# A decoder layer on one core: the order of evictions in the first batch, and centring in two parts

## The chip, the cores and the metric

The kernel runs on one core of a Trainium2 chip. The metric is the device time in microseconds (us) of one execution; the median of three runs of the kernel before is 1821.55 us (1820.07 to 1822.1). The engines are TensorE (PE, matrix products), VectorE (DVE), ScalarE (ACT), GpSimd (POOL) and SyncE (SP), which here only issues DMA transfers. Each engine works through its own list of instructions in order; they wait for each other by semaphores.

## The reference

Eight batches of 512 tokens of 512 values each (`x`), with a context of the same shape:

```python
x = x + attn(layernorm(x), queries, combiners)              # heads of 128, no softmax
x = x + xattn(layernorm(x), ctx, ctx, Wq,bq, Wk,bk, Wv,bv)  # softmax attention over the context
x = x + ffn(layernorm(x), router, experts, shared mlp)      # 16 experts, top 2, capacity 640
```

The first attention has no softmax, so `out_h = X_h @ (Q_h . (X^T X) . C)`: with `G = X^T X`, a 512x512 matrix per batch, the kernel forms `T = G C`, `M = Q T` and `A = X M`. In the cross attention Wq and Wk are multiplied once (`W = Wq Wk^T`), so scores are `(y1 W) ctx^T`; values are `V = ctx Wv`.

## The kernel before, in words

Phase 1 does both attentions batch by batch, phase 2 the shared MLP and the experts. The change touches phase 1 only (`phase1`, from L108). Work is cut into named steps, and one list `order` (L1244 to L1275) gives for every iteration i the steps of batches i and i+1 in the order in which every engine goes through them: Y1T, V (values), ST0, LN0, MEAN, STORE, LN2, Q, Y2, G, T, SC (scores), M, PT (turned probabilities), C (context), A, LN1, PV. Iteration -1, which begins the kernel, has a list of its own (L1257). Each engine has a `step(name, b)` that issues its part of a step. Where an engine has no part, the step's place in the list says nothing for it.

Most products are made in three passes (`three_pass`, L63): each operand is split into a high part (a copy rounded by ACT) and a low part (the difference, by DVE or POOL), and high-high, high-low, low-high are summed: 12 matmuls of 128x512 for one output tile. Tiles stand in the 8 PSUM banks by the table BANK (L123). `filled` waits until PE has filled a bank; `drained` waits until a bank's eviction is done (semaphores `s_ev`), which for a split product is DVE's instruction.

First batch, up to batch 0's Q. W is made in four columns (INIT to INIT3, L1026); for each, ACT copies the high part into WH (L599) and DVE makes the low part (L794). C: ACT copies the context's four chunks to `ch` (L672, shown at the helper's line L527), DVE makes `cl` (L805), for b = 0; for later batches POOL makes it (L469). M: four times eight matmuls, ACT evicts (L570). A: 32 matmuls of 128x128 (L1145) in four tiles, in banks 6, 7, 0, 1; DVE evicts each at L831 and adds x. Then DVE takes statistics (L735), deviations (L724 to L753), and ACT normalises to y (L532, step LN1). V: four tiles of 12 matmuls (L72) in banks 5, 6, 7, 4. V's group waits at L1038 to L1043 before its first tile: for the last W bank, for `cl`, and for the third eviction of A (`drained(pe, "A", b, 2)`). ACT copies each tile to `vh` (`value_hi`, L688), DVE makes `vl` (`residual`, L843, at L846). Y1T: PE turns y (L1007), ACT copies to `y1h` (L604), DVE makes `y1l` (L885). Q: four tiles (L72), in the same banks as V, whose first tile waits for `y1l` chunk by chunk, and whose tile c waits for V's tile c. Step KEY (POOL L457, ACT L582, then two small transfers by SP) makes a row that DVE uses at L765 behind Y1T; ST0(1) and LN0(1) follow, and G(1) on PE waits for them.

Centring. For each batch `centre` (L296) takes the tokens' means from the turned tokens `xT`, in four instructions (L303), one for each chunk; each waits for `s_xT` (the load) and `s_mrow` (the row of means, written to DRAM and read back, L343 and L351). For batch 0 DVE does it, later POOL, in step MEAN. A(b) waits on PE for all four (L1138). In POOL's list, MEAN(b+2) follows PV(b). In PV(b) POOL adds y2 to x (L480), then for each of four token tiles t copies the two halves of the words of y2 (L491) into one of two buffers, `halves(b, t)`, t modulo 2, so tile 2 waits until the store of tile 0 has landed, and tile 3 for tile 1 (L488). SP stores each (L394) as it is ready, and after all four issues the turning of the first two probability tiles (L400, from `p_planes` that ACT writes), and the load of x (L402). The turned probabilities pass through DVE (L921) and ACT, in step M and PT, and DVE makes their low part (`p_lo`, L783) between the evictions of A; PV's first two tiles on PE wait for it (L1163). ACT copies M behind `p_top`, the first half of one of them (L567). POOL's L469 (step C) runs at that time. DVE's L914, in SC, is an addition of one column between the maximum of a tile of scores (L912) and the bias for its exponential (L648).

Of the kernel before, what the change touches and what calls it, by code (L numbers as in the profile page):

```python
# [40 lines left out]
B, S, D = 8, 512, 512  # L41
# [66 lines left out]
def phase1(nc, ctx, a, Y, shared, at):  # L108
# [123 lines left out]
        return y1_words[:, :, t * P:(t + 1) * P].bitcast(U16).rearrange("p c (n two) -> p c n two", two=2)  # L232

    ph, pl = y1h, y1l
    P_BY_DMA = 2
    p_planes = [at(44 + t, [2, D], U16) for t in range(P_BY_DMA)]
    p_turned = [at(row, [2 * NC, P], U16) for row in (12, 43)]
# [55 lines left out]
    s_ct_hi, s_ct_lo, s_ct_stored, s_ct_loaded = (sem(f"s_ct_{k}") for k in ("hi", "lo", "stored", "loaded"))  # L293
    s_g_hi = sem("s_g_hi")

    def centre(eng, b):  # L296

        eng.wait_ge(s_xT, 16 * (b + 1))
        eng.wait_ge(s_mrow, 16 * (b + 1))
        by_tile = mean_row[:].rearrange("q (p t) -> q t p", t=NT)  # L300
        for c in range(NC):
            tokens = xT[:, c, :].rearrange("q (t p) -> q t p", t=NT)
            eng.tensor_tensor(tokens, tokens, by_tile, ALU.subtract).then_inc(s_centred, 1)  # L303

# [101 lines left out]
    def gpsimd(pool):  # L406
# [39 lines left out]
        def step(name, b):  # L446
            if name == "MEAN":
                if b >= 1:
                    centre(pool, b)
            if name == "FILL":  # L450
                pool.wait_ge(s_small, 16 * 3)
                fill_tables()
# [18 lines left out]
            if name == "PV":  # L471
                if b == 0:
                    pool.wait_ge(s_pad, 32)
                if b < B - 2:
                    pool.wait_ge(s_stat[0], b + 3)
                else:
                    drained(pool, "V", b + 1, 0)
                for t in range(NT):
                    pool.wait_ge(s_y2, NT * b + t + 1)
                    pool.tensor_tensor(x[b % XS][:, t, :], x[b % XS][:, t, :], y2[:, t, :],  # L480
                                       ALU.add).then_inc(s_base, 1)
                if b == B - 1:
                    pool.wait_ge(s_ttop, NT)
                    pool.wait_ge(s_tlow, NT)
                for t in range(NT):
                    n = NT * b + t
                    if n >= 2:
                        pool.wait_ge(s_yout[t % 2], 16 * (n // 2))  # L488
                    words = y2[:, t, :].bitcast(U16).rearrange("p (d two) -> p d two", two=2)
                    for half in range(2):  # L490
                        last = pool.tensor_copy(halves(b, t)[:, half, :], words[:, :, 1 - half])  # L491
                    last.then_inc(s_halves, 1)
            if name == "LN1" and b in BY_DMA:
                filled(pool, "PT", b - 1, NT - 1)
                for t in range(NT):
                    pool.wait_ge(s_y1, NT * b + t + 1)
                    words = y[:, t, :].bitcast(U16).rearrange("p (d two) -> p d two", two=2)
                    for half in range(2):
                        last = pool.tensor_copy(y1_planes[t][:, half, :], words[:, :, 1 - half])
                    last.then_inc(s_planes, 1)  # L500
# [24 lines left out]
    def scalar(act):  # L525
# [25 lines left out]
        def step(name, b):  # L551
# [136 lines left out]
            def value_hi(t):  # L688
                filled(act, "V", b, t)
                bank = bank_of("V", b, t)  # L690
                copy(vh[:, t, :], bank[:]).then_inc(s_vh, 1)

            if name == "V" and b in BY_DMA:
                filled(act, "PV", b - 1, NT - 1)
                for t in range(NT):
                    y1_words_of(t)
                    if t >= 1:
                        y1_hi(t - 1)
                    if 0 < t < NT - 1:
                        value_hi(t - 1)  # L700
                y1_hi(NT - 1)
                for t in range(2, NT):
                    value_hi(t)
            else:
                for t in value_tiles(name, b):
                    value_hi(t)
                    if t == 1 and b == B - 1:
                        normalise_x2(b - 1)

# [2 lines left out]
    def vector(dve):  # L712
# [75 lines left out]
        def step(name, b):  # L788
# [60 lines left out]
            if name == "V":  # L849
                if b == B - 1:  # L850
                    for t in value_tiles(name, b):
                        residual(t)
                if b >= 1:
                    key_row_ready(b)
                for t in range(NT - 1):
                    if b >= 1:
                        key_row_and_statistics(b, t)
                if b in BY_DMA:
                    for t in range(2, NT):
                        dve.wait_ge(s_y1_turned[t], 16 * b)  # L860
                        dve.tensor_copy(word_halves(t)[:, :, :, 0], y1_turned[t][:, NC:2 * NC, :])\
                           .then_inc(s_low_dve, 1)
                    for t in range(NT):
                        cols = slice(t * P, (t + 1) * P)
                        dve.wait_ge(s_y1h, NC * b + t + 1)
                        dve.tensor_tensor(y1l[:, :, cols], y1_words[:, :, cols], y1h[:, :, cols].bitcast(F32),
                                          ALU.subtract).then_inc(s_ev["Y1T"], 1)
                        if t == 1:
                            residual(0)
                elif b < B - 1:  # L870
                    residual(0)
                if b >= 1:
                    key_row_and_statistics(b, NT - 1)
                    key_row_bias(b)
                if b < B - 1:
                    for t in range(1, NT):
                        residual(t)
            if name in LATE:
                residual(LATE[name])
            if name == "Y1T" and b not in BY_DMA:  # L880
                for c in range(NC):
                    dve.wait_ge(s_y1h, NC * b + c + 1)
                    y1_filled(dve, b, c)
                    bank = bank_of("Y1T", b, c)
                    dve.tensor_tensor(y1l[:, c, :], bank[:], y1h[:, c, :].bitcast(F32), ALU.subtract)\  # L885
                        .then_inc(s_ev["Y1T"], 1)
            if name == "LOW":
                for q in range(H):
                    dve.wait_ge(s_ct_hi, q + 1)
# [108 lines left out]
    def tensor(pe):  # L998
# [23 lines left out]
        def step(name, b):  # L1022
# [13 lines left out]
            if name == "V":  # L1036
                if b == 0:
                    pe.wait_ge(s_wh, NC + 1)  # L1038
                    drained(pe, "W", 0, NC - 1)
                pe.wait_ge(s_cl, NC * (b + 1))  # L1040
                if b not in BY_DMA:
                    drained(pe, "PV", b - 1, 3)
                drained(pe, "A", b, 2)  # L1043
            if name in LATE:
                drained(pe, "Q", b, LATE[name] - 2)
            if name == "V" or name in LATE:
                for t in value_tiles(name, b):
                    if b in BY_DMA and t == NT - 1:
                        drained(pe, "PV", b - 1, 3)
                    cols = slice(t * P, (t + 1) * P)  # L1050
                    parts = [(ch[:, c, cols], cl[:, c, cols], VWH[:, c, :], VWL[:, c, :]) for c in range(NC)]
                    three_pass(pe, bank_of("V", b, t)[:], parts).then_inc(s_mm["V"], 1)
# [121 lines left out]
def phase2(nc, ctx, a, Y, shared, at, attn):  # L1174
# [70 lines left out]
    for i in range(-1, B):  # L1245
# [9 lines left out]
        if i == -1:  # L1255

            steps = [("ST0", 0), ("LN0", 0), ("WV", 0), ("INIT", 0), ("MEAN", 0), ("G", 0), ("INIT1", 0), ("T", 0),  # L1257
                     ("C", 0), ("INIT2", 0), ("M", 0), ("INIT3", 0), ("KEY", 0), ("FILL", 0), ("A", 0), ("LN1", 0)]
            steps.append(("V", 0))
        if i == 0:  # L1260
            steps.remove(("V", 0))
# [461 lines left out]
```

## Time and profile before

| | |
|---|---|
| median of 3 runs | 1821.55 us (1820.07 to 1822.1) |
| the profiled execution's own time | 1821.36 us |
| its span | 1819.6 us |
| PE busy | 1805.0 us, 99% |
| DVE, ACT, POOL busy | 874.2 (48%), 799.2 (44%), 920.4 (51%) |
| granted clock of PE | 0.998 of full speed over the span |
| chain that ended last | PE 96%, DVE 1%, DMA 1% |

The span is the time from the profile's first to its last instruction; the execution's own time has 1.76 us around it. All times below are microseconds from the span's start unless marked ns. In a row of a timeline, several like instructions in a row stand as one, with their count; its second number is the time from the first one's start to the last one's end. Instructions of an engine are pipelined, so the end of one may lie behind the start of the next. `L527` is the helper `copy` of ACT, whatever it copies; `L72` is any product in three passes.

### The profile page before, as it was taken

How to read it: one execution, taken by the hardware profiler on the slowest of the kernel's cores; microseconds unless marked ns; L12 is line 12 of the kernel's file. 1: busy time of each engine (PE TensorE's matmuls, PEld its weight loads, DVE VectorE, ACT ScalarE, POOL GpSimd, SP SyncE). 2: the span in 40 equal slices, each digit the busy share in tenths (PEclk: the TensorE clock that was granted, in tenths of full speed). 3: DMA queues.
4: the chain of work that ended last, by engine and by line, in shares of the span. 5: the costliest groups of instructions: out<-in, count | busy, mean ns of one | idle time of the engine just before them, and what ended most of it. 6: DMA issues, size and time to landing. Idle time of an engine off the chain costs nothing.

```text
span 1819.6 us, 27098 instructions
## 1 busy us (share of the span) xinstructions
PE 1805.0 (99%) x9960; PEld 1598.3 (88%) x9960; DVE 874.2 (48%) x2064; ACT 799.2 (44%) x1574; POOL 920.4 (51%) x808
## 2 busy tenths in 40 slices
PE   9999999999999999999999999999999999999997
PEld 6888888888887878888999999999999999999996
DVE  6668777787745444332444323443343423443242
ACT  4555556555544343332444434444344433444331
POOL 3454564546653232225665656556665556656531
PEclk9999999999999999999999999999999999999999
DMA  8454545443552333224666676666666666666722
GB/s 319 147 133 123 151 140 151 134 141 97 147 114 42 47 54 68 36 41 93 173 140 131 163 155 134 139 146 161 147 140 128 161 152 140 144 134 163 155 31 29
DMA packets 254292, 229.34 MB, mean 126 GB/s; under 512 B 171697, under 2 KB 171697, under 8 KB 252881
## 3 DMA queue, kind: packets, MB, share of 16 engines
q1 hardware_dynamic: 228864, 174.51, 36.2%
q0 software_dynamic: 25296, 53.11, 17.4%
q8 instruction: 79, 1.29, 0.3%
q14 instruction: 53, 0.43, 0.1%
HBM read 138.80 MB, written 49.97 MB: 104 GB/s over the span
## 4 chain that ended last, share of the span: by engine, by line
PE 96%; DVE 1%; DMA 1%; issue 0%; ACT 0%; SPq 0%; POOL 0%; DVEq 0%; ACTq 0%; POOLq 0%
PE ps L72 67%; PE ps L1668 23%; PE ps L1001 4%; PE ps L1145 1%; PE ps L1007 1%; DMA buffer<-means 0%; DMA buffer<-in_x 0%; DMA means<-mean 0%; DVE buffer L831 0%; ACT buffer L1478 0%; DVE buffer L303 0%; PE ps L1081 0%; DVE buffer L783 0%; ACT buffer L527 0%; DVE buffer L794 0%
## 5 line engine op out<-in xcount | busy, mean ns | idle before, releaser
L72 PE MATMUL ps<-buffer,buffer 128*128 128x320 f32 (+1 forms) x6900 | 1239.2, 341 | 1.3 <-DVE buffer L831 0.8
L72 PEld LDWEIGHTS ps<-buffer,buffer 128*128 128x128 f32 x6900 | 1120.9, 188 | 107.6 <-issue 1.5
L1420 POOL TENSOR_TENSOR buffer<-buffer,buffer 128x512 fp32r<-128x512 f32 x289 | 380.4, 1483 | 252.3 <-ACT buffer L1478 252.0
L1668 PE MATMUL ps<-buffer,buffer 128*128 128x512 f32 x1904 | 437.4, 390 | 0.4 <-DVE buffer L1611 0.4
L1668 PEld LDWEIGHTS ps<-buffer,buffer 128*128 128x128 f32 x1904 | 356.0, 188 | 74.3 <-DVE buffer L1611 0.8
L1520 ACT ACTIVATE buffer<-ps 128x320 f32<-128x320 f32 (+1 forms) x240 | 112.5, 469 | 600.1 <-PE ps L72 600.0
L1478 ACT ACTIVATE buffer<-buffer 128x512 fp32r<-128x512 f32 (+1 forms) x491 | 293.2, 651 | 163.1 <-PE ps L1668 91.8
L1586 DVE TENSOR_TENSOR ps<-ps,buffer 128x320 f32<-128x320 f32 (+2 forms) x198 | 100.2, 506 | 488.8 <-ACT buffer L1520 488.8
L1467 POOL DMA_INDIRECT out_tokens<-buffer,slot_list x80 | 125.8, 1573 | 185.5 <-DVE buffer L1616 177.8
L519 POOL DMA_INDIRECT slots<-pairs,slot_u x64 | 63.6, 993 | 181.7 <-DVE slot_u L988 164.7
L527 ACT ACTIVATE buffer<-buffer 128x512 fp32r<-128x512 f32 (+1 forms) x212 | 126.5, 681 | 20.4 <-DMA buffer<-buffer 15.1
L1616 DVE TENSOR_SCALAR buffer<-ps,slot_list 128x512 f32<-128x512 f32 x80 | 59.7, 747 | 112.1 <-PE ps L1668 112.1
L532 ACT ACTIVATE buffer<-buffer,shift,rstd 128x512 f32<-128x512 f32 x96 | 70.3, 804 | 94.5 <-DVE shift L753 94.5
L1570 DVE TENSOR_TENSOR buffer<-ps,buffer 128x320 fp32r<-128x320 f32 (+2 forms) x198 | 96.6, 488 | 10.0 <-ACT buffer L1478 9.0
L1433 POOL DMA_INDIRECT buffer<-tokens_normed,slot_list x80 | 83.5, 1044 | 29.3 <-issue 29.3
L510 POOL TENSOR_TENSOR buffer<-buffer,buffer 128x512 f32<-128x512 f32 x32 | 40.5, 1294 | 103.0 <-DVE shift L753 99.1
L1478 ACT ACTIVATE buffer<-ps 128x320 fp32r<-128x320 f32 (+2 forms) x198 | 86.3, 436 | 0.7 <-DVE ps L1586 0.7
L527 ACT ACTIVATE buffer<-ps 128x512 fp32r<-128x512 f32 (+2 forms) x124 | 63.9, 557 | 44.4 <-PE ps L72 34.0
L1586 DVE TENSOR_TENSOR buffer<-ps,buffer 128x512 f32<-128x512 f32 (+1 forms) x42 | 29.0, 690 | 101.1 <-ACT buffer L1520 101.0
L1554 DVE COPY buffer<-buffer 128x512 uint16<-128x512 uint16 x80 | 73.6, 942 | 0.5
L735 DVE BATCH_NORM_STATS2 stats<-buffer 128x6 f32<-128x512 f32 x96 | 61.0, 680 | 7.8 <-DMA buffer<-in_x 7.7
L469 POOL TENSOR_TENSOR buffer<-buffer,buffer 128x512 fp32r<-128x512 f32 x28 | 38.4, 1403 | 37.7 <-ACT buffer L527 37.7
(131 smaller groups left out, 1090.8 us busy)
## 6 DMA issues: line engine op xcount, KB each, us to landing
buffer<-in_wts SPq DMA_DIRECT2D x289, 256.0 KB, 3.0
buffer<-in_xT SPq DMA_DIRECT2D x8, 1024.0 KB, 5.5
buffer<-in_ctxT SPq DMA_DIRECT2D x8, 1024.0 KB, 8.4
out_tokens<-buffer SPq DMA_DIRECT2D x8, 1024.0 KB, 4.3
tokens_normed<-buffer SPq DMA_DIRECT2D x32, 256.0 KB, 3.1
out_tokens<-buffer POOLq DMA_DIRECT2D x32, 256.0 KB, 6.7
buffer<-in_x SPq DMA_DIRECT2D x7, 1024.0 KB, 5.6
buffer<-combiners_top SPq DMA_DIRECT2D x6, 1024.0 KB, 5.0
```

Source lines behind the costliest of these rows:

```text
L72: last = pe.matmul(out, left, right, start=(c == 0 and i == 0), stop=(c == len(parts) - 1 and i == 2))
L527: return act.activation(dst, src, ACT.Copy)
L1001: last = pe.matmul(out, left, right, start=(i == 0), stop=(i == len(pairs) - 1))
L1420: pool.tensor_tensor(wl[n % RING][:], wraw[n % RAW][:], wh[n % RING][:].bitcast(F32), ALU.subtract).then_inc(s_wl, 1)
L1433: pool.indirect_dma_start(xn[:, t, :], None, Y[:, :], rows_at(groups[g][1], t), bounds_check=N + PAD - 1).then_inc(s_xg, 16)
L1467: pool.indirect_dma_start(out[:, :], rows_at(part, t), ost[:, t, :], None, bounds_check=N + PAD - 1, compute_op=ALU.add).then_inc(s_add[t] ...
L1478: return act.activation(dst, src, ACT.Copy)
L1520: act.activation(silu[u % TMP][0:rows_of(c), 0:n], bank[0:rows_of(c), 0:n], ACT.Silu)\
L1554: dve.tensor_copy(halves_of(t)[:, :, :, 0], xp[t][:, NC:2 * NC, :]).then_inc(s_xlow, 1)
L1570: dve.tensor_tensor(lo[:, first:first + n], product_of(u)[0:rows, 0:n], hh[0:rows, c, first:first + n].bitcast(F32), ALU.subtract).then_in ...
L1586: dve.tensor_tensor(product_of(u)[0:rows_of(c), 0:n], up_bank[u % 2][rows, 0:n], silu[u % TMP][0:rows_of(c), 0:n], ALU.mult).then_inc(s_ht, 1)
L1668: ins = pe.matmul(down_bank[n % 2][:], left, right, start=(c == 0 and i == 0), stop=(c == FC - 1 and i == len(passes) - 1))
```

## The change

Five edits, all in phase 1:

1. In the first list, C(0) moves from behind T(0) to behind M(0). On ACT, the copies of W's third column and of M now come ahead of the context's four; DVE's `cl` come behind the low part of W's third column.
2. PE's V(0) no longer waits for A's third eviction before its first tile; tile t > 0 waits for A's eviction t - 1. (The other condition is rewritten and means the same.)
3. V(0)'s last tile: ACT's copy and DVE's residual move from V(0) to the end of Y1T(0), behind the four copies and four low parts of the turned tokens.
4. POOL's centring of batch b+2, for b = 0 to 5: its first two chunks move into PV(b), behind the copies of halves of tile 1.
5. The other two stay in MEAN(b+2).

```diff
@@ phase1
+    CENTRED_EARLY, CENTRED_LATE = range(2), range(2, NC)
...
-    def centre(eng, b):
+    def centre(eng, b, chunks=range(NC)):
         eng.wait_ge(s_xT, 16 * (b + 1))
         eng.wait_ge(s_mrow, 16 * (b + 1))
         by_tile = mean_row[:].rearrange("q (p t) -> q t p", t=NT)
-        for c in range(NC):
+        for c in chunks:
...
@@ gpsimd step
             if name == "MEAN":
                 if b >= 1:
-                    centre(pool, b)
+                    centre(pool, b, CENTRED_LATE if b >= 2 else range(NC))
...
                     last.then_inc(s_halves, 1)
+                    if t == 1 and b + 2 < B:
+                        centre(pool, b + 2, CENTRED_EARLY)
@@ scalar step
+            if name == "Y1T" and b == 0:
+                value_hi(NT - 1)
...
                 for t in value_tiles(name, b):
-                    value_hi(t)
+                    if (b, t) != (0, NT - 1):
+                        value_hi(t)
@@ vector step
                 if b < B - 1:
-                    for t in range(1, NT):
+                    for t in range(1, NT if b > 0 else NT - 1):
                         residual(t)
...
             if name == "Y1T" and b not in BY_DMA:
...
                         .then_inc(s_ev["Y1T"], 1)
+                if b == 0:
+                    residual(NT - 1)
@@ tensor step
                 pe.wait_ge(s_cl, NC * (b + 1))
-                if b not in BY_DMA:
+                if b == B - 1:
                     drained(pe, "PV", b - 1, 3)
-                drained(pe, "A", b, 2)
+                if b > 0:
+                    drained(pe, "A", b, 2)
...
                         drained(pe, "PV", b - 1, 3)
+                    if b == 0 and t > 0:
+                        drained(pe, "A", b, t - 1)
@@ phase2, the list of steps for i == -1
-                     ("C", 0), ("INIT2", 0), ("M", 0), ("INIT3", 0), ("KEY", 0), ("FILL", 0), ("A", 0), ("LN1", 0)]
+                     ("INIT2", 0), ("M", 0), ("C", 0), ("INIT3", 0), ("KEY", 0), ("FILL", 0), ("A", 0), ("LN1", 0)]
```

## Rows read from the trace of the kernel before

**Rows 1.** page, part 1: busy us, share of the span, instructions

```profile
PE 1805.0 (99%) x9960; PEld 1598.3 (88%) x9960; DVE 874.2 (48%) x2064; ACT 799.2 (44%) x1574; POOL 920.4 (51%) x808
```

**Rows 2.** PE timeline, first batch: start, us, what, [idle before <-who ended it]

```profile
29.11 1.02 PE L1026 MATMUL ps<-buffer,buffer 128*128 128x512 f32 x2
...
30.55 3.84 PE L1145 MATMUL ps<-buffer,buffer 128*128 128x128 f32 x32 [0.42 <-ACT buffer L527]
...
35.21 11.16 PE L72 MATMUL ps<-buffer,buffer 128*128 128x512 f32 x48 [0.82 <-DVE buffer L831]
...
46.22 1.91 PE L1007 MATMUL ps<-ident,buffer 128*128 128x128 f32 x16
...
48.48 11.13 PE L72 MATMUL ps<-buffer,buffer 128*128 128x512 f32 x48 [0.36 <-DVE buffer L885]
```

**Rows 3.** PE timeline, batches 2 to 7

```profile
143.38 32.92 PE L72 MATMUL ps<-buffer,buffer 128*128 128x512 f32 x144
...
198.65 3.81 PE L1145 MATMUL ps<-buffer,buffer 128*128 128x128 f32 x32 [0.72 <-issue]
...
202.21 32.91 PE L72 MATMUL ps<-buffer,buffer 128*128 128x512 f32 x144
...
260.16 32.92 PE L72 MATMUL ps<-buffer,buffer 128*128 128x512 f32 x144
...
376.21 32.94 PE L72 MATMUL ps<-buffer,buffer 128*128 128x512 f32 x144
...
434.18 11.59 PE L72 MATMUL ps<-buffer,buffer 128*128 128x512 f32 x48
```

**Rows 4.** ACT timeline, first batch

```profile
27.34 2.19 ACT L527 ACTIVATE buffer<-buffer 128x512 fp32r<-128x512 f32 x4 [2.03 <-DMA buffer<-in_ctxT]
...
29.44 1.55 ACT L527 ACTIVATE buffer<-ps 128x512 fp32r<-128x512 f32 x3
...
44.14 1.54 ACT L527 ACTIVATE buffer<-ps 128x512 fp32r<-128x512 f32 x3
...
55.81 2.94 ACT L532 ACTIVATE buffer<-buffer,shift,rstd 128x512 f32<-128x512 f32 x4 [1.71 <-DVE shift L753]
```

**Rows 5.** DVE timeline, first batch

```profile
29.41 2.48 DVE L805 TENSOR_TENSOR buffer<-buffer,buffer 128x512 fp32r<-128x512 f32 x4
...
33.01 2.71 DVE L831 SCALAR_TENSOR_TENSOR buffer<-ps,rstd,buffer 128x512 f32<-128x512 f32 x4
...
44.82 1.89 DVE L846 TENSOR_TENSOR buffer<-ps,buffer 128x512 fp32r<-128x512 f32 x3 [1.24 <-ACT buffer L527]
...
47.65 2.48 DVE L885 TENSOR_TENSOR buffer<-ps,buffer 128x512 fp32r<-128x512 f32 x4
```

**Rows 6.** POOL timeline, batches 1 to 7

```profile
183.72 2.28 POOL L491 COPY buffer<-buffer 128x512 uint16<-128x512 uint16 x4
...
189.30 1.17 POOL L491 COPY buffer<-buffer 128x512 uint16<-128x512 uint16 x2 [3.30 <-DMA tokens_normed<-buffer]
...
192.35 6.20 POOL L303 TENSOR_TENSOR buffer<-buffer,buffer 128x512 f32<-128x512 f32 x4
...
376.17 4.35 POOL L469 TENSOR_TENSOR buffer<-buffer,buffer 128x512 fp32r<-128x512 f32 x3 [4.31 <-ACT buffer L527]
...
421.49 2.29 POOL L491 COPY buffer<-buffer 128x512 uint16<-128x512 uint16 x4 [2.71 <-DMA tokens_normed<-buffer]
...
434.14 5.51 POOL L469 TENSOR_TENSOR buffer<-buffer,buffer 128x512 fp32r<-128x512 f32 x4 [4.38 <-ACT buffer L527]
```

**Rows 7.** DVE timeline ahead of the probabilities' product, batches 3, 6, 7

```profile
197.74 1.12 DVE L921 COPY buffer<-buffer 128x512 uint16<-128x512 uint16 x1 [0.55 <-DMA buffer<-buffer]
...
377.43 0.69 DVE L783 TENSOR_TENSOR buffer<-buffer,buffer 128x512 fp32r<-128x512 f32 x1
...
435.52 1.72 DVE L783 TENSOR_TENSOR buffer<-buffer,buffer 128x512 fp32r<-128x512 f32 x1
```

**Rows 8.** line L914: engine op xcount: ns min/median/max, first and last start

```profile
L914 DVE TENSOR_TENSOR mr<-smax,krow x32: 158/506/1391, 66.7 to 475.7; 128x1 f32<-128x1 f32 x32
```

## The prediction

> **What bounds the kernel now.** I read the page first: TensorE (PE) is busy for 99% of the span, so only time in which PE stands still, or work added to it, can move the result [rows 1]. Next the PE timeline of the first batch. A row's bracket is the idle time in front of it and who ended it; the reader is to see three small holes: attention's product A(0) starts at 30.55 with 0.42 of idle behind ScalarE (ACT), V(0) at 35.21 with 0.82 behind VectorE's evictions of A at L831, and, with the transposes of Y1 at 46.22 right behind V, Q(0) at 48.48 with 0.36 behind VectorE (DVE) at L885 [rows 2]. "Idle" understates a hole, since an end in the trace overlaps the next start: the 32 matmuls of A start 35.21 - 30.55 = 4.66 us before V, and without a wait they take 3.6 (from 198.65 to 202.21, 3.56 [rows 3]), so this hole is worth 1.1 us. In the PE timeline of the later batches I compare the starts of the 144-matmul block behind A: 143.38, 202.21, 260.16, and two batches later 376.21 [rows 3]. Steps: 58.83, 57.95, and 116.05 for two. Against 57.95 the step into batch 3 is 0.88 too long and the last pair 0.15 too long. The 0.88 stands in front of A(3), 0.72 of it as idle time at 198.65. Who ended it, the view doesn't say; the GpSimd (POOL) timeline does: its four centring instructions of batch 3 run from 192.35 for 6.20, to 198.55, and A waits for them [rows 6]. They were late because the copies of halves at L491 sat 3.30, and once more, behind stores to DRAM. In the other batches that gap is 2.7, as in the row at 421.49 [rows 6], and the centring is in time. Last the ACT and DVE timelines of the first batch [rows 4, 5], for the durations.
>
> **First batch.** Times are the trace's; a prime marks my estimate.
> M's copy ahead of the context's. Before, ACT makes the four copies of the context from 27.34 for 2.19, and only then the evictions of WH's third column, M and WH's fourth, three from 29.44 at about 0.5 each [rows 4]. PE gives M just ahead of the row at 29.11, so ACT can take M at 29.3', ends it at 29.9', and PE, with two matmuls from 29.11 (0.94 from start to start), starts A(0) at 30.05' in place of 30.55. Gain 0.5 at this point.
> Its cost: the context's copies start at 29.85' in place of 27.34. DVE works without a hole from the first of four L805 at 29.41, 0.62 each, through two L794 to the evictions of A at 33.01 [rows 5]. Now one L794 goes first, to 30.03', then DVE waits until the first copy is there at 30.45', so everything behind it is 0.42 later: L805 ends at 32.9', the last L794 at 33.5', the evictions of A start at 33.43'. Nothing else is moved past ACT here: WH's fourth column is copied at 32.05', before DVE asks for it. POOL's KEY products wait for the last L805 and so start 1 us later; DVE asks for what they feed behind Y1's low parts, near 50. SP issues nothing in the moved step for this batch.
> V waits for single evictions. V's first tile has a bank of its own; it now waits only for the split context (32.9') and the last W bank (33.5'), both of which hide behind A's matmuls, which end at 30.05 + 3.6 = 33.65'. V starts at 33.7' in place of 35.21, 1.5 us earlier. Its second tile waits for the first eviction of A, done at 34.1', and asks at 36.4': hidden.
> What is late next. V ends at 44.7', and the tokens normalised on ACT, which hang on the DVE chain (evictions, statistics, deviations) and so come 0.42 later, are ready at 44.7' too. The transposes start at 44.8' in place of 46.22 and end at 46.6'. Then Q(0) needs the first low part of the turned tokens (L885). Before, DVE reached L885 at 47.65, having waited for V's last tile; now that tile is out of the way, and DVE comes to L885 straight from three residuals at L846, which took 1.89 from 44.82: 44.82 + 0.42 + 3 x 0.61 = 47.07' [rows 5]. ACT is ahead of it: three evictions of V from 44.14 at 0.5 each, then the high part, at 46.7' [rows 4]. From L885's start to Q's start it was 0.83 (47.65 to 48.48), so Q(0) starts at 47.9': **gain 0.58**. So of 1.5 us won at V, 0.9 goes back in front of Q, where DVE is the engine that ends the wait.
> V's last tile behind the turned tokens moves one ACT and one DVE instruction (0.6 each) behind four of Y1. Q's fourth tile needs that bank 8 us after Q starts; DVE is at it by 50.2'. The chain towards batch 1 (ST0, then LN0 on ACT at 55.81 [rows 4]) has the same instructions as before, less 0.34 of waiting, plus 0.42: it is 0.08 later. G(1) on PE asks for its result at 58.9' and it is there at 58.8 + 0.08 = 58.9': no hole, or one of 0.1. I bound the first batch from 0.1 (the copies come later than I think, or DVE's chain is stretched once more) to 0.8 (DVE's wait of 0.42 is not there), and take 0.55.
>
> **Centring in two parts.** Nothing is added, but two of four POOL instructions (1.55 each, 3.1 together) go between the two pairs of halves' copies. There POOL stood still for 2.7 to 3.3 us [rows 6]. Behind them on POOL are the copies of halves 2 and 3, then the late centring, then the context's low parts for the next batch, which wait for ACT anyway. In batches with a gap of 2.7 the halves come up to 0.35 later; for these SP waits, and after them SP issues the turning of the probabilities (L400) and a load of x. Centring then ends 2.7 earlier, in batch 3 a full 3.1 earlier, at 195.4'. A(3) starts as soon as M's copy is there: the 0.88 goes.
> What is late next in batch 3: the turned probabilities. They hang on the same late halves, which the change does not move. DVE copies the second of them at 197.74, behind a DMA [rows 7], it lasts 0.66 without POOL beside it, and so DVE's work of A(3), which elsewhere starts about 0.25 behind A's start, starts 0.6 behind A's new start at 197.8'. That ends in the low part of the turned probabilities, L783. Batch 7 shows what a small delay does there: POOL's L469, 5.51 / 4 = 1.38 each, run from 434.14 [rows 6], L783 starts 1.38 behind, at 435.52, and takes 1.72 in place of 0.69 [rows 7], and PE's 48 matmuls behind it took 11.59 where the same 48 take 11.13 at 48.48 [rows 2, 3]. So this costs 0.45. In batch 6, undisturbed, L783 starts at 377.43 [rows 7], 1.26 behind POOL's first L469 at 376.17 [rows 6], so 0.12 ahead of the second, and wins; 0.35 later it loses. I take this as given back in batch 3: **0.88 - 0.45 = 0.43**; with both ends, 0.88 and 0.3.
> The 0.15 before batch 6: one-column additions on DVE (L914) last 158 ns alone and up to 1391 beside POOL [rows 8]; the last of them holds up the fourth exponential, and that, on ACT, M's copy. The late centring now ends before it. **Gain 0.15**, or none.
> Batch 7's hole of 0.45 I leave where it is: the DVE work ahead of L783 was 0.1 longer there, beside loads of weights which stay.
>
> **A rule that speaks against the change.** The rows say that a small DVE instruction stretched to nearly the length of one POOL instruction [rows 8]. The Trainium skill ("SBUF — State Buffer", Who interferes with whom) says that a DVE instruction with two SBUF inputs contends with a GpSimd instruction that reads SBUF, and that the one which started first keeps the port for its whole length. By this rule, moving 3.1 us of POOL work earlier only changes which DVE instructions wait, up to 1.5 us each, and what that can cost here is rival (c), worked out there from rows; the trace's 158 and 1391 ns agree with it, and without it the sum stays the same.
>
> **Sum.** 0.55 + 0.43 + 0.15 = 1.1 us. The profiled execution took 1821.36 (span 1819.6, 1.76 around it), 0.19 under the median 1821.55, so I count from it: 1821.36 - 1.1 = 1820.2 us.
>
> **Rivals.**
> (a) DMA latency in batch 1 was chance. The 3.30 against 2.7 elsewhere speaks for it, and so does the spread of the runs, 1820.07 to 1822.1. Then batch 3 has no late transposes in this execution, the whole 0.88 goes, or there was none in the other runs to win. With it 1.6 is gained on this trace: 1819.8.
> (b) Batch 7's hole goes too, since the centring that slowed DVE's copies just ahead of it has ended: 1.1 + 0.45 = 1.55 gained, 1819.8; together with (a) 1819.3.
> (c) The other side: the later halves. If 0.35 more at the halves reaches L783, or the early centring delays DVE's second maximum and through it the planes, then DVE loses to POOL's second L469 in each of batches 2 to 7: six times 0.45 is 2.7, less the one that is there already, 2.25, against 0.55 + 0.88 + 0.15 = 1.58 gained: 1821.36 + 0.7 = 1822.0. It decides from a shift of 0.12 at L783's start. For it: the small margin. Against: in these batches I found no wait of DVE for the transposes, and nothing else on DVE between A's start and L783 hangs on the halves.
> (d) The first batch gives nothing, as DVE's 0.42 becomes 1.0 (a context copy held up): 1820.7.
>
> **How the numbers follow.** Forecast 40%, (a) or (b) 30%, (c) 15%, (d) and smaller mishaps 15%. The cases go from 1819.3 to 1822.0; widened by about half of what the three runs scatter (2.03), more below, where the lowest run lay 1.5 under the median,, the range is 1818.4 to 1822.3; the likeliest case's own is 1819.5 to 1821.0. A change of 0.2% is 3.6 us, about what a measurement of this kernel can tell from none: no case reaches it, so same gets 0.93, faster 0.04, slower 0.03, for mechanisms that I haven't seen.
>
> **What would show it.** A(0) at about 30.05 and V(0) at 33.7 with no idle before them; Q(0) at 47.9 with over 1 us of idle in front, ended by DVE at L885; DVE's L805 starting near 30.45. POOL: two L303 between the pairs of L491, and two behind. A(3) without idle, PE's steps 57.95 everywhere, and L783 long in batches 3 and 7. I am wrong if V still starts near 35, if Q(0) does not move, if POOL's early part waits for the means' row (then halves and stores slide), or if L783 is long in every batch.

## The result and the profile after

| | before | after |
|---|---|---|
| median of 7 runs | 1821.55 us (1820.07 to 1822.1) | 1833.91 us (1825.02 to 1836.81) |
| profiled execution, its span | 1821.36, 1819.6 | 1833.42, 1831.7 |
| ratio | | 1.006, 95% interval 1.0046 to 1.0073 |

The kernel became slower by 0.6%, where I had forecast 1.1 us less. It also scatters more: two of seven runs lie at 1825.0 and 1826.9, the others from 1833 up, and the profiled one is one of those.

PE timeline of the changed kernel, first batch and the start of each 144-matmul block, columns as in [rows 2, 3]. `L1009` is what L1001 was before, `L1015` L1007, `L1034` L1026, `L1156` L1145, `L837` L831, `L891` L885, `L922` L914, `L304` L303, `L492` L491, `L789` L783, `L771` L765, `L530` L527, `L535` L532, `L651` L648, `L458` L457, `L438` L437.

```profile
30.23 3.83 PE L1156 MATMUL ps<-buffer,buffer 128*128 128x128 f32 x32
...
33.92 11.16 PE L72 MATMUL ps<-buffer,buffer 128*128 128x512 f32 x48
...
45.03 1.97 PE L1015 MATMUL ps<-ident,buffer 128*128 128x128 f32 x16
...
48.19 11.16 PE L72 MATMUL ps<-buffer,buffer 128*128 128x512 f32 x48 [1.20 <-DVE buffer L891]
...
63.99 5.79 PE L1009 MATMUL ps<-buffer 128*128 128x128 f32 x32 [4.64 <-ACT buffer L535]
...
92.06 32.90 PE L72 MATMUL ps<-buffer,buffer 128*128 128x512 f32 x144
...
150.59 33.16 PE L72 MATMUL ps<-buffer,buffer 128*128 128x512 f32 x144
...
208.87 33.37 PE L72 MATMUL ps<-buffer,buffer 128*128 128x512 f32 x144
...
268.70 33.11 PE L72 MATMUL ps<-buffer,buffer 128*128 128x512 f32 x144
...
328.35 33.11 PE L72 MATMUL ps<-buffer,buffer 128*128 128x512 f32 x144
...
387.99 33.13 PE L72 MATMUL ps<-buffer,buffer 128*128 128x512 f32 x144
```

And the one row of before that answers to 92.06 there:

```profile
85.44 32.90 PE L72 MATMUL ps<-buffer,buffer 128*128 128x512 f32 x144
```

Read it in two parts. **The first batch.** A(0), V(0) and the transposes start earlier, as meant, and Q(0) at 48.19 in place of 48.48. Then G(1) comes at 63.99 (before: 59.44) behind 4.64 of idle, and its 32 matmuls take 5.79, where they took 3.73 before; the block that began at 85.44 begins at 92.06, **6.62 later**. **The later batches.** The steps are 58.53 (to 150.59), 58.28, 59.83, 59.65 and 59.64 against 57.95 undisturbed: 6.2 over, where the kernel before had 0.88 + 0.15 over in the same stretch [rows 3]. Together that is 11.8 of the 12.1 between the spans.

**Why G(1) waits.** The chain of waits of the changed kernel, 28 to 72 (start, us, what):

```profile
39.21 4.94 DMA key_row<-key_sums
...
44.16 10.94 DMA buffer<-key_row
...
55.23 0.48 DVE buffer L771
...
61.01 2.94 ACT buffer L535 x4
...
63.99 5.79 PE ps L1009 x32
```

DVE's row products (L771) need the key row, which goes to DRAM and back on SP's queue. SP and POOL timelines of the changed kernel, then both of the kernel before:

```profile
39.21 0.33 SPq L360 DMA_DIRECT2D key_row<-key_sums  x1
...
44.16 0.33 SPq L362 DMA_DIRECT2D buffer<-key_row  x1
```

```profile
33.37 5.05 POOL L458 TENSOR_TENSOR buffer<-buffer,buffer 128x512 f32<-128x512 f32 x4 [30.15 <-DVE buffer L811]
...
38.37 1.11 POOL L438 DMA_DIRECT2D tokens_normed<-buffer  x1
...
39.48 0.93 POOL L438 DMA_DIRECT2D out_tokens<-buffer  x1
```

```profile
37.83 0.33 SPq L359 DMA_DIRECT2D key_row<-key_sums  x1
...
40.37 0.33 SPq L361 DMA_DIRECT2D buffer<-key_row  x1
```

```profile
32.05 5.00 POOL L457 TENSOR_TENSOR buffer<-buffer,buffer 128x512 f32<-128x512 f32 x4 [28.83 <-DVE buffer L805]
...
38.22 1.11 POOL L437 DMA_DIRECT2D tokens_normed<-buffer  x1 [1.17 <-DMA rw<-in_rw]
```

Before, the small store of the sums is issued at 37.83, ahead of POOL's fill of the padding (two stores of 1280 KB, from 38.22; POOL has waited 1.17 for a load, `rw`, ahead of them), lands in 2.5 us and the load goes out at 40.37. After, POOL's key products start at 33.37 instead of 32.05, the store goes out at 39.21, behind the fill's first store at 38.37, and lands after 4.94; the load goes out at 44.16 and takes 10.94 in place of 7.7. The row lands at 55.1, 7 us later than before (48.1), and takes away all the margin that hid it.

**Why G(1) is slow, too.** Windows of the changed kernel (length, then busy time of PE, PE's weight loads, DVE, ACT and POOL, then the granted clock of TensorE, DMA share and GB/s):

```profile
59.00:64.00 5.00, 0.36 (x3) 0.01 (x1) 3.99 (x14) 2.99 (x5) 0.00 (x0) 0.73 0.37 37
...
64.00:69.50 5.50, 5.50 (x31) 5.50 (x32) 2.73 (x4) 2.23 (x4) 3.93 (x3) 0.62 1.03 397
```

PE had stood still for 4.6 us; the granted clock is 0.73 in the window of the wait and 0.62 in the one behind it, between its two levels of 1.2 and 2.4 GHz, and 1.00 again from 69.5. That is 5.79 - 3.73 = 2.06 us more for 32 matmuls, on top of the wait.

**Why the later batches lose 1.7 each.** DVE, POOL, PE and ACT timelines of batch 4's scores (A(5) follows):

```profile
314.31 5.48 DVE L922 TENSOR_TENSOR mr<-smax,krow 128x1 f32<-128x1 f32 x1
...
320.67 0.16 DVE L922 TENSOR_TENSOR mr<-smax,krow 128x1 f32<-128x1 f32 x1
...
325.19 0.47 DVE L929 COPY buffer<-buffer 128x512 uint16<-128x512 uint16 x1 [2.70 <-DMA buffer<-buffer]
...
330.10 1.09 DVE L789 TENSOR_TENSOR buffer<-buffer,buffer 128x512 fp32r<-128x512 f32 x1
```

```profile
311.50 3.07 POOL L304 TENSOR_TENSOR buffer<-buffer,buffer 128x512 f32<-128x512 f32 x2
...
314.49 2.30 POOL L492 COPY buffer<-buffer 128x512 uint16<-128x512 uint16 x4
...
316.73 3.05 POOL L304 TENSOR_TENSOR buffer<-buffer,buffer 128x512 f32<-128x512 f32 x2
```

```profile
323.42 1.09 PE L1015 MATMUL ps<-ident,buffer 128*128 128x128 f32 x8 [0.86 <-ACT buffer L651]
```

```profile
320.07 0.69 ACT L651 ACTIVATE buffer<-ps,nbias 128x512 f32<-128x512 f32 x1 [6.76 <-DVE nbias L923]
...
323.90 1.67 ACT L530 ACTIVATE buffer<-ps 128x512 f32<-128x512 f32 x5
```

The addition of one column (L922, `mr`), 159 ns alone, took 5.48: it came up at 314.31, and ended with the last of POOL's run, 316.73 + 3.05 = 319.78; the other long ones end with a run of POOL too, to 0.03 us. Before, with a pause of 2.7 us in the run, none of 32 took over 1391 ns [rows 8]. The exponentials behind it come late (320.07), so do the planes, their turning, M's copy on ACT (323.90) and A; PE waits 0.86 for the last exponential before it turns the other two tiles at 323.42. Four additions are so long; the steps into batches 4, 5 and 6 are 1.9, 1.7 and 1.7 over (0.46 of the first lies in batch 3's block, see below), and the one into batch 2, where the addition took 4.57, is 0.6 over. Each long addition also costs 0.2 to 0.3 behind its block's start, which falls into the next step: DVE's second low part (L789) takes 1.1 in place of 0.7, and the 144 matmuls 33.1 in place of 32.9.

### The profile page after: what moved, and what is told of

Same layout as the page of the kernel before. It is cut to its first block, busy times and chain, and to the rows that moved or that the text cites. A ratio compares the mean times of both kernels' runs of the same rounds, so it can differ in the third digit from the quotient of the medians.

```text
span 1831.7 us, 27103 instructions
## 1 busy us (share of the span) xinstructions
PE 1810.9 (99%) x9960; PEld 1600.1 (87%) x9960; DVE 879.4 (48%) x2064; ACT 797.7 (44%) x1574; POOL 918.9 (50%) x808
## 4 chain that ended last, share of the span: by engine, by line
PE 89%; DVE 4%; DMA 2%; POOL 2%; ACT 2%; issue 1%; SPq 0%; ACTq 0%; DVEq 0%; POOLq 0%
PE ps L72 60%; PE ps L1679 23%; PE ps L1009 3%; DVE mr L922 1%; PE ps L1156 1%; PE ps L1034 1%; DMA buffer<-buffer 1%; ACT buffer L530 1%; DMA buffer<-key_row 1%; POOL buffer L481 1%; PE ps L1015 0%; DVE stats L741 0%; DVE buffer L837 0%; POOL buffer L492 0%; ACT buffer L651 0%
## 5 line engine op out<-in xcount | busy, mean ns | idle before, releaser
L530 ACT ACTIVATE buffer<-buffer 128x512 fp32r<-128x512 f32 (+1 forms) x212 | 126.5, 681 | 18.2 <-DMA buffer<-buffer 15.0
L535 ACT ACTIVATE buffer<-buffer,shift,rstd 128x512 f32<-128x512 f32 x96 | 70.4, 805 | 101.0 <-DVE shift L759 101.0
L530 ACT ACTIVATE buffer<-ps 128x512 fp32r<-128x512 f32 (+2 forms) x124 | 63.9, 557 | 48.8 <-PE ps L72 32.8
```

The source lines that it names most:

```text
L530: return act.activation(dst, src, ACT.Copy)
L535: act.activation(dst[:, t, :], x[b % XS][:, t, :], ACT.Identity, bias=shift[k][:, t:t + 1], scale=rstd[k][:, t:t + 1]).then_inc(done, 1)
```

## Experiments

Medians stand beside the kernel before on the same chip; intervals are of the ratio. Only split_only, first_only and move_only lie clear of no change; every gain in the table reaches 1.0 with its interval. Each kernel has one trace.

| kernel | median us | before | difference | ratio, 95% |
|---|---|---|---|---|
| split_only | 1826.04 | 1821.24 | +4.8 | 1.0027 (1.0017 to 1.0037) |
| first_only | 1828.05 | 1821.24 | +6.8 | 1.0027 (1.0014 to 1.004) |
| first_fill_late | 1821.01 | 1821.24 | -0.2 | 0.9999 (0.9989 to 1.0009) |
| split_column | 1820.51 | 1821.24 | -0.7 | 0.9996 (0.9986 to 1.0006) |
| v_without_move | 1819.62 | 1820.93 | -1.3 | 0.9994 (0.9985 to 1.0004) |
| move_only | 1828.00 | 1820.93 | +7.1 | 1.0042 (1.0027 to 1.0058) |
| early_first | 1821.59 | 1820.93 | +0.7 | 1.0006 (0.9996 to 1.0015) |
| v_split_column | 1818.83 | 1820.93 | -2.1 | 0.9991 (0.9982 to 1.0) |
| all_mended | 1820.30 | 1820.81 | -0.5 | 0.9997 (0.9988 to 1.0007) |
| column_only | 1820.49 | 1820.81 | -0.3 | 0.9998 (0.9989 to 1.0007) |
| v_column | 1819.53 | 1820.81 | -1.3 | 0.9993 (0.9984 to 1.0002) |
| early_one | 1820.49 | 1820.92 | -0.4 | 0.9997 (0.9988 to 1.0007) |

**The two halves of the change.** split_only is the kernel before with edits 4 and 5, first_only with edits 1 to 3.

> Only the centring in two parts is taken from the change; the first batch is as before. Theory S (DVE starves): with the 2.7 us gap between the copies of halves filled, POOL runs 7.6 us without a pause, and DVE's one-column addition with two SBUF inputs, if it comes up in it, waits for the end of the whole run; in three or four of batches 2 to 7 it lasts about 5 us, and PE loses 1.7 us in each. Time 1825 to 1828, and no long addition in batch 3, where the stores leave POOL pauses. Rival L (the late halves of my prediction): additions of at most 1.5 us, L783 long instead, 1822 at most. Rival F: all the loss of the change comes from the first batch; then this is within 1 us of before.

> Only the three edits of the first batch. Theory K (the key row): POOL's key products start 1.3 us later, so the key row's small store is issued behind POOL's fill of the padding (2.6 MB) instead of ahead of it, and its two transfers take 16 us in place of 10; DVE, and with it G(1), waits for the row some 4.6 us, and PE then runs its 32 matmuls in 5.8 in place of 3.7 us at a lower granted clock. Time 1821.5 + 6 = 1827 to 1829. Rival: the loss in the first batch was chance of one execution, and the median is 1821 (gain of 0.55 as predicted).

Both lose, 4.8 and 6.8, and the sum, 11.6, is close to what the whole change loses (12.4, on another chip). In split_only the longest addition took 5530 ns (engine op xcount: ns min/median/max):

```profile
L917 DVE TENSOR_TENSOR mr<-smax,krow x32: 158/353/5530, 66.4 to 480.0; 128x1 f32<-128x1 f32 x32
```

Three of them are over 5 us, ahead of A(5), A(6) and A(7); theory S holds, and L and F fall. Of the ten runs of first_only four lie at 1821.6 to 1823.4 and six at 1828.0 to 1831.3: I read that as a race between the row's store and the fill, but have a trace of only one execution, a late one: store at 38.98, fill at 38.12. In the three late traces with the moved copies (the change, first_only, move_only) the fill starts right behind POOL's key products, 0.83 to 0.86 ahead of the store; in the traces with the old order it first waits for the load of `rw` and starts at 37.3 to 38.5. What puts an early run right is not shown. The two quick runs of the whole change (1825.0, 1826.9) lie where split_only's do (1824.8 to 1827.5), as if only the second cause were in them.

**The fill moved out of the way.**

```diff
-   ("KEY", 0), ("FILL", 0), ("A", 0), ...
+   ("KEY", 0), ("A", 0), ...
...
-   steps.insert(1, ("QBIAS", 0))
+   steps[1:1] = [("QBIAS", 0), ("FILL", 0)]
```

> The three edits of the first batch, and POOL's fill of the padding moved behind its products for the queries' bias, so that it cannot stand ahead of the key row. Theory K: the row's two transfers take 5 to 8 us, G(1) does not wait, no fall of the clock: Q(0) near 48.2, time 1820.5 to 1821.3. Rival Q (the row's transfers are slow by themselves or because of the other loads): the row still lands behind 52 and the time stays near 1828. A new wait is possible: G's low part waits for the fill's end, about 60.

SP timeline, then PE's:

```profile
38.74 0.33 SPq L359 DMA_DIRECT2D key_row<-key_sums  x1
...
41.06 0.33 SPq L361 DMA_DIRECT2D buffer<-key_row  x1
```

```profile
47.72 11.13 PE L72 MATMUL ps<-buffer,buffer 128*128 128x512 f32 x48 [1.19 <-DVE buffer L888]
...
58.69 3.78 PE L1006 MATMUL ps<-buffer 128*128 128x128 f32 x32
```

The store goes out as late as in the change (38.74) and lands in 2.3, the load takes 5.1, and G(1) starts at 58.69 without a wait or a slow stretch. All ten runs lie from 1820.73 to 1822.26. So the cause of the wait is the fill ahead of the row on the DMA queues, not the lateness itself. The new wait that I feared for G's low part does not appear.

**The addition without a second SBUF tensor.**

```diff
-   dve.tensor_tensor(mr[:, t:t + 1], smax[:, t:t + 1], krow[:, t:t + 1], ALU.add)
+   dve.tensor_scalar(mr[:, t:t + 1], smax[:, t:t + 1], krow[:, t:t + 1], None, ALU.add)
```

> Centring in two parts, and DVE's addition L914 written as a tensor-scalar instruction, whose second operand is a per-partition scalar and not a second SBUF tensor. Theory S: the addition lasts 0.2 us everywhere, whatever POOL does, and the 1.7 us holes go; time 1820.3 to 1821.2. Rival G (any DVE instruction starves in POOL's unbroken run, or PE waits for the later halves): the holes stay, 1825 to 1828.

```profile
L917 DVE TENSOR_SCALAR mr<-smax,krow x32: 213/214/216, 66.4 to 475.5; 128x1 f32<-128x1 f32 x32
```

With POOL's run as unbroken as in split_only, the addition takes 213 to 216 ns, all 32 of them, and the time falls by 5.5 us, to 1820.51. Theory S holds as to the instruction: it is the form with two SBUF tensors that starves. The Trainium skill ("SBUF — State Buffer", Who interferes with whom) says that a DVE instruction with two SBUF inputs contends with a GpSimd instruction that reads SBUF, and that one with at most one SBUF input, outside DVE's two-port modes, does not; the 5530 and 216 ns agree. It also says that the loser is blocked for the whole instruction of the other; here it was blocked for up to 5.5 us, over several instructions of 0.6 to 1.5 us each, and the measurement decides. In this trace batch 3 still has a hole of 0.60 before A(3), which waits for ACT, and 0.4 behind it at the low part: the step there is 58.75.

**Which of the first batch's edits loses.** v_without_move has edits 2 and 3 only, move_only edit 1 only:

```diff
-   ("C", 0), ("INIT2", 0), ("M", 0), ("INIT3", 0)
+   ("INIT2", 0), ("M", 0), ("C", 0), ("INIT3", 0)
```

> The first batch's second and third edit (V's tiles wait for single evictions, V's last tile behind the turned tokens) without the first: the context's copies stay ahead of M's. By theory K all of the loss there comes from the first edit, which delays POOL's key products; here they stay where they were. A(0) at 30.6 as before, V(0) at 34.2, and DVE reaches Y1's low parts 0.4 us earlier than in the change (46.7), so Q(0) at 47.5: gain 0.9 to 1.0, median 1820.2 to 1820.6, no run above 1823. Rival: the row's lateness comes from the edits of V, and runs near 1828 stay.

> The first edit alone (M's copy ahead of the context's). Theory K: the key row's store is issued behind the fill, the row lands near 53 to 55, G(1) waits, runs near 1828 with a few near 1822. Rival: alone it costs 0.4 (DVE's chain is later by that much), 1821.7.

v_without_move: V(0) at 34.31, Q(0) at 47.40, ten of its eleven runs from 1819.35 to 1821.3. The eleventh took 2572.24, with a mean granted clock of 0.654 where the others have 0.998; why, I don't know. No run is near 1828, as theory K has it. The median is 1.3 under before, where 0.9 to 1.0 was expected; the 0.3 are within the interval.

move_only loses 7.1 (four runs only, 1826.1 to 1829.07). As theory K has it, the store goes out at 38.77 behind the fill at 37.94, and the row lands at 54.8. But K is not all of it. PE timeline of its profiled execution (1826.1, the quickest of the four), then a window:

```profile
35.57 12.78 PE L72 MATMUL ps<-buffer,buffer 128*128 128x512 f32 x48 [1.88 <-DVE buffer L831]
...
63.65 3.84 PE L1001 MATMUL ps<-buffer 128*128 128x128 f32 x32 [2.07 <-ACT buffer L532]
```

```profile
36.00:42.00 6.00, 6.00 (x21) 4.74 (x20) 5.48 (x23) 2.04 (x7) 5.68 (x8) 0.72 0.42 139
```

With V's old wait for the third eviction of A, the later evictions hold V(0) up: 1.88 of idle, then a granted clock of 0.72 from 36 to 42 (1.00 before and behind), and V's 48 matmuls take 12.78 in place of 11.16. Q(0) is at 50.45, 2 us late before the row plays any part; in front of G(1), 2.07 more.

**Where the early part stands.** early_first puts it ahead of all copies of halves, so that POOL's pause stays; early_one leaves it where the change has it, but with one instruction of four:

```diff
# early_first
+   if b + 2 < B:
+       centre(pool, b + 2, CENTRED_EARLY)
    for t in range(NT):
        n = NT * b + t
# early_one
+   CENTRED_EARLY, CENTRED_LATE = range(1), range(1, NC)
```

> Centring in two parts, the early part ahead of the copies of halves of tile 0 instead of behind those of tile 1, so that POOL's pause of 2.7 us stays. Theory S: the second tile's addition, which starved, now comes up in or near the pause and lasts under 1.5 us; the first tile's addition comes up in a run of 10 us and may last 3 to 5 us, but its exponential has 4 us to spare, so PE does not wait: 1820.3 to 1821.8. Rival: any long unbroken run costs PE, 1824 or more.

> As split_only, but one centring instruction (1.5 us) goes ahead instead of two, and three stay behind; the addition is the old one with two SBUF inputs. POOL then still stands still for about 1.2 us between the copies of halves, in place of 2.7 before and 0 in split_only. Theory S, pause form (what lets DVE in is a pause of POOL): no addition lasts over 1.6 us, time 1820.8 to 1822. Rival (what matters is how much is put ahead of the copies, or the order centring, copies, centring): additions of 4 us and more remain, 1824 to 1828.

early_first: no addition over 1517 ns, so the starving is gone, first tile included, against my 3 to 5 us for it. But it is not faster than before: PE waits 0.41 before A(3) and 0.99 before A(7), both for ACT. early_one, POOL timeline and the additions:

```profile
301.61 1.58 POOL L304 TENSOR_TENSOR buffer<-buffer,buffer 128x512 f32<-128x512 f32 x1
...
304.39 2.28 POOL L492 COPY buffer<-buffer 128x512 uint16<-128x512 uint16 x4 [1.21 <-DMA tokens_normed<-buffer]
```

```profile
L917 DVE TENSOR_TENSOR mr<-smax,krow x32: 159/516/1419, 66.3 to 474.4; 128x1 f32<-128x1 f32 x32
```

A pause of 1.21 is enough: the longest addition is 1419 ns, and the time 1820.49, 0.3 under the range expected. In batch 3 of the changed kernel, pauses of 0.28 and 0.76 among the copies of halves were there, and no addition took over 1.14. With early_one and split_only differing in one centring instruction's place, the pause form of theory S holds in these traces. Why DVE gets in between two instructions of POOL where eight follow each other, as in the kernel before, and at times does not where sixteen do (L481, L492, L304, L492, L304), I can't say; it stays open.

**Together, and a better version.** all_mended is the whole change with both mends. column_only is the kernel before with the new addition. v_column has the new addition and edits 2 and 3; v_split_column adds the split to it.

> The whole change with both mends: the fill behind the queries' bias, and the addition as tensor-scalar. If the two causes (key row behind the fill, DVE starving in POOL's run) are all of the loss, this is at or below before: 1820.0 to 1821.0. Rival: a third cause is left when both parts stand together, over 1822.

> The kernel before with the addition as tensor-scalar and nothing else. My prediction's 0.15 before batch 6 should be won by this alone: 1820.6 to 1821.0. Rival: no difference, since no such addition was on the path.

> V's two edits and the addition as tensor-scalar, without the split of the centring. It tells what the split is worth once nothing starves. If it wins the hole before A(3), 0.5 or more: v_column is at 1819.4 and v_split_column at 1818.9. Rival: batch 3's hole is the late turned probabilities in either form, and both are within 0.2 of each other.

> V's two edits without the move, centring in two parts and the addition as tensor-scalar: a version meant to beat both. Sum of the single parts: 0.95 from the first batch, 0.7 from centring with the addition (as measured, 1820.51 against 1821.24): 1819.3 to 1820.0. If the parts share what they win, 1820.3.

all_mended at 1820.30, as expected: no third cause. column_only moves 0.3, within the interval of no change. v_column at 1819.53 and v_split_column at 1818.83 are where expected of this pair. v_split_column is the fastest, 2.1 us under before and 15.1 under the change, which ran on another chip. PE timeline:

```profile
46.55 11.17 PE L72 MATMUL ps<-buffer,buffer 128*128 128x512 f32 x48 [0.21 <-DVE buffer L891]
...
141.53 32.92 PE L72 MATMUL ps<-buffer,buffer 128*128 128x512 f32 x144
...
199.57 32.91 PE L72 MATMUL ps<-buffer,buffer 128*128 128x512 f32 x144
```

The sum of parts that I expected was 0.5 too high. The step to batch 3's block is 58.04, 0.09 over. Q(0) at 46.55 says less than it seems: v_without_move and v_column have the same first batch and Q(0) at 47.40 and 47.63, and this execution was 0.9 to 1.1 earlier from the start. v_column, without the split, keeps a hole of 0.81 before A(3) and is 1.3 under before; so the split is worth 0.8 here, though the two stood on different chips and their intervals overlap.

## Why the prediction was wrong

**M's copy and V's waits: the working held, the row that it started from was not typical.** Counted from the start of the two matmuls ahead of A(0) (29.11 before, 29.37 in this execution), A(0), V(0) and Q(0) stand 0.86, 4.55 and 18.82 behind; the prediction comes to 0.94, 4.59 and 18.79, the kernel before to 1.44, 6.10 and 19.37. So 0.55 was won at Q(0) against that trace, where I had 0.58. But that trace is the slowest of its kind:

| first batch | traces | A(0) behind the two matmuls | Q(0) behind them |
|---|---|---|---|
| as before | before, column_only, split_only, split_column, early_first, early_one | 0.86 to 1.93 | 18.45 to 19.37, mean 18.85 |
| edits 1 to 3 | after, first_only, first_fill_late, all_mended | 0.86 | 18.81 and 18.82 |
| edits 2 and 3 | v_without_move, v_column, v_split_column | 1.30 to 1.35 | 17.99 to 18.05 |

Against the mean, all three edits together win nothing at Q(0), and edits 2 and 3 alone win 0.8. The hole of 0.42 before A(0) hangs on ACT's wait for the load of the context (2.03 in the trace of before [rows 4]); in column_only that wait was 1.37, and A(0) had no hole without any move:

```profile
29.30 1.02 PE L1026 MATMUL ps<-buffer,buffer 128*128 128x512 f32 x2
...
30.16 3.83 PE L1145 MATMUL ps<-buffer,buffer 128*128 128x128 f32 x32
```

Edit 1 costs 0.8 at Q(0) even before the key row (first_only against v_without_move, 18.81 and 17.99): it makes DVE's chain later, and DVE ends PE's wait there, 1.2 with the move and 0.2 without. The 0.55 was a gain over one execution.

**"POOL's KEY products ... start 1 us later; DVE asks for what they feed behind Y1's low parts, near 50": this is the step that failed first, by 6.6 us.** I followed the products and not what SP issues behind them. The store and load of the row had their lengths in the trace of before, 2.5 and 7.7, landing at 48.1, two us ahead of the need; and POOL's fill stood 0.4 us behind the store. A step 1.3 us later crossed it, and two transfers that had taken 10.2 took 15.9. Priced by the trace: 4.6 of wait, and 2.06 by the clock. So also "it is 0.08 later. G(1) ... no hole": the hole was 4.64. My bound for the first batch, 0.1 to 0.8 gained, left the queue out. With the fill out of the way (first_fill_late) the wait is gone, and the time is 0.2 under before, which is no change.

**"Centring in two parts. Nothing is added": the second failure, 5.6 of the 6.2 us by which five steps of the trace are over.** POOL's pause of 2.7 us was not idle time to be used; it was where DVE's two-input instructions got through. I had read 158 and 1391 ns, took one POOL instruction as the price of a meeting, and rival (c), which had the right place ("the early centring delays DVE's second maximum") had the wrong price: 0.45 at L783 instead of 1.7 to 1.9 by an addition of 5.4 us. The Trainium skill's rule that I weighed gave the same bound of one instruction, and its bound was too low too.

**Batch 3: about right.** Undisturbed (all_mended), the block starts 8.02 behind the row of 32 matmuls ahead of the transposes, before it was 8.89. PE timeline of the changed kernel, then of the kernel before, where the block starts at 202.21 [rows 3]:

```profile
200.78 3.73 PE L1009 MATMUL ps<-buffer,buffer 128*128 128x128 f32 x32
...
205.28 3.84 PE L1156 MATMUL ps<-buffer,buffer 128*128 128x128 f32 x32
```

```profile
193.32 3.73 PE L1001 MATMUL ps<-buffer,buffer 128*128 128x128 f32 x32
```

208.87 - 200.78 = 8.09: A(3) is 0.07 late, and the rest of the step's 0.33 is batch 2's longer block. Then the 144 matmuls take 33.37 against 32.91, the 0.46 given back at the low part. So 0.80 - 0.46 = 0.34 was won, where I had 0.43. It varies from trace to trace. In the seven traces without the split the block of batch 3 starts 0.75 to 1.52 late, so the hole was not chance (rival (a)); in the five with the early part as in the change, 0.00 to 0.78, and in three of them 0.4 to 0.5 more is given back. In split_column it was 0.78, behind the turned tiles on ACT (M's copy stands behind `p_top`), a wait that I had not looked at. The 0.66 that I took for DVE's copy "without POOL beside it" is wrong: POOL's centring ran beside that copy too, and free of it the copy takes 0.46; I had the chain there longer than it is.

**Batches 6 and 7.** 0.15 before batch 6 cannot be told under the starving. One of the steps into batches 4 to 6 is 0.13 to 0.16 over in four traces with the old addition (before, first_only, early_first, early_one); in the five with the new one none is over 0.02, but for the 0.42 of split_column's low part. So the term may be right; column_only's 0.3 is not beyond its interval.

**The chances.** I gave 0.03 to slower by over 0.2%, as none of my cases reached 3.6 us. All cases were sums of holes of 0.1 to 1 us seen in the trace; the two that happened were margins used up, which no row of idle time on PE shows. The upper end of the range was also set closer than the lower: 0.3 above the worst case, where half of the scatter is 1.0. It would not have reached the result.

## What to carry to other kernels

When a step moves later, follow it through every transfer that it issues, and look at what stands just behind it on the other engines' DMA queues: here a 2 KB store that slipped behind a fill of 2.6 MB cost far more than the move could win. Do not fill an engine's pause before you know who uses it: here, POOL's pause was what let DVE's addition of two SBUF tensors in; with its second operand given as a per-partition scalar first, the pause could be filled. Take edits that look independent apart on the chip before adding them up: here one of the first three lost 7 us and hid the other two's gain of about 1. And read a hole of half a microsecond in more than one trace before pricing it: five other traces of the same first batch would have said that the 0.55 was not there to win.

## What the runs showed of the hardware that I had not expected

A DVE instruction of 159 ns on one column lasted up to 5530 ns beside POOL, across several POOL instructions, in unbroken runs; with a pause of 1.2 us ahead of the second part of the run, at most 1419. The same addition as tensor-scalar took 211 to 216 ns, all 160 of them in five traces. A wait of 4.6 us on PE was followed by 5.5 us at a mean granted clock of 0.62, which cost 2.06 us on 32 matmuls of 128x128. In move_only a wait of 1.88 us was followed by a mean of 0.72 over 6 us, which cost 1.62 us on 48 matmuls of 128x512. The 2 KB store took 2.1 to 2.5 us ahead of the fill of 2 x 1280 KB or without it, and 4.3 to 4.9 behind its first store; the load of 256 KB after it 5.0 and 5.1 with no fill beside it, and 10.9 to 12.0 behind a late store.
